# A fused token-mixing tower: in-block sums written by VectorE into the PSUM tile that TensorE accumulates, instead of being added by a permutation matmul

## The reference, cut to what matters

```
def step(state, qkv_t):
    q_t, k_t, v_t = qkv_t
    hebbian = jnp.einsum('bhi,bhj->bhij', v_t, k_t)
    state = retention[None] * state + Gamma[None] * hebbian
    y_t = jnp.einsum('bhij,bhj->bhi', W_static[None] + state, q_t)
    return (state, y_t)
...
h = _L0_tok_ref(x, ...)
h = h + _L0_attn_ref(_layernorm(h, axis=-1), ...)
h = h + _L0_ffn_ref(_layernorm(h, axis=-1), ...)
```

## Time and profile before

| | us |
|---|---|
| median of 3 runs (255.31 to 257.43) | 257.43 |
| the profiled execution, own time | 258.98 |
| its span in the trace | 257.1 |
| TensorE busy (granted clock 0.98 on the mean) | 227.3 |
| VectorE busy | 198.4 |
| GpSimd busy | 186.8 |
| ScalarE busy | 108.0 |

### The profile page before, as it was taken

One profiled execution on the slowest core, in us unless ns is written; L12 is line 12 of the kernel. 1 busy time (PEld: TensorE's weight loads), 2 busy tenths in 40 slices (PEclk: granted clock), 3 DMA queues, 4 the chain that ended last, 5 costly groups with the idle time before them and its releaser, 6 DMA issues.

```text
span 257.1 us, 7827 instructions
## 1 busy us (share of the span) xinstructions
PE 227.3 (88%) x3266; PEld 168.3 (65%) x3266; DVE 198.4 (77%) x391; ACT 108.0 (42%) x272; POOL 186.8 (73%) x97
## 2 busy tenths in 40 slices
PE   5998886998889999999989999998987965868993
PEld 5978644775558586776757767676554853547992
DVE  1027975688966896899799977887899989895773
ACT  6303674135522222697831056977102367100230
POOL 5870009999989999998599995776999999400031
PEclk9999999999999999999999999999999996899998
DMA  5492027411053921101640620025406100110002
GB/s 154 133 273 101 0 84 205 164 45 43 3 146 87 258 88 45 43 1 43 187 145 3 179 70 3 1 72 160 143 3 201 49 4 1 43 41 3 0 3 82
DMA packets 19443, 21.26 MB, mean 83 GB/s; under 512 B 2416, under 2 KB 13904, under 8 KB 19408
## 3 DMA queue, kind: packets, MB, share of 16 engines
q1 hardware_dynamic: 18640, 18.65, 23.3%
q0 software_dynamic: 768, 2.11, 3.4%
HBM read 14.98 MB, written 5.77 MB: 81 GB/s over the span
## 4 chain that ended last, share of the span: by engine, by line
PE 69%; DVE 13%; issue 6%; ACT 4%; DMA 3%; POOL 2%; another core or an unknown queue 1%; SPq 0%; DVEq 0%; ACTq 0%; POOLq 0%
PE y_ps L1127 10%; PE scr L978 10%; PE w_ps L1110 8%; PE scr L955 6%; PE q_ps L1072 5%; PE scr L992 5%; PE scr L1007 4%; PE scr L968 4%; PE scr L932 3%; PE y_ps L1072 3%; DVE zz L896 3%; PE scr L1031 3%; PE scr L1045 3%; POOL uu L447 2%; PE y_ps L1121 2%
## 5 line engine op out<-in xcount | busy, mean ns | idle before, releaser
L447 POOL TENSOR_TENSOR uu<-vg,kk 128x1024 f32<-128x1024 f32 x64 | 150.8, 2392 | 32.0 <-DMA vg<-v_far 19.3
L896 DVE TENSOR_TENSOR zz<-e_hg,q_ps 128x1524 f32<-128x1524 f32 x32 | 55.3, 1728 | 0.0
L867 DVE TENSOR_TENSOR_SCAN e_hg<-decay,w_ps 128x512 f32<-128x512 f32 x32 | 39.0, 1218 | 10.3 <-PE w_ps L1110 9.8
L1110 PE MATMUL w_ps<-uu,comb 128*32 128x128 f32 x1024 | 35.3, 277 | 1.5 <-POOL uu L447 1.1
L1110 PEld LDWEIGHTS w_ps<-uu,comb 128*32 128x32 f32 x1024 | 27.5, 111 | 9.0 <-issue 7.9
L1127 PEld LDWEIGHTS y_ps<-zz,coll 128*32 128x32 f32 x768 | 19.8, 111 | 19.4 <-issue 8.7
L1127 PE MATMUL y_ps<-zz,coll 128*32 128x128 f32 x768 | 28.2, 281 | 4.7 <-DVE zz L896 4.7
L406 POOL TENSOR_TENSOR tok_dom<-tok_dom,bf 128x1024 f32<-128x1024 f32 x4 | 8.7, 2186 | 21.0 <-DVE tmp_b L710 21.0
L527 ACT ACTIVATE junk<-tok_dom 128x256 bf16<-128x256 f32 x24 | 9.7, 407 | 28.6 <-DVE tok_dom L664 28.6
L882 DVE TENSOR_TENSOR zz<-e_hg,q_ps 128x512 f32<-128x512 f32 x32 | 21.7, 679 | 0.0
L396 POOL DMA_INDIRECT tok_dom<-in_table,ids_sb x16 | 15.5, 969 | 6.2 <-issue 3.5
(11 more groups left out here) (124 smaller groups left out, 390.5 us busy)
## 6 DMA issues: line engine op xcount, KB each, us to landing
vg<-v_far SPq DMA_DIRECT2D x32, 256.0 KB, 4.2
v_far<-v_sb SPq DMA_DIRECT2D x8, 256.0 KB, 4.0
out_h<-tok_dom SPq DMA_DIRECT2D x8, 256.0 KB, 2.1
k_far<-kk SPq DMA_DIRECT2D x12, 128.0 KB
k_sb<-k_far SPq DMA_DIRECT2D x4, 384.0 KB, 3.2
wexp<-in_w_exp SPq DMA_DIRECT2D x1, 256.0 KB
tok_dom<-in_table,ids_sb POOLq DMA_INDIRECT x16, 5.0
wproj<-in_w_proj SPq DMA_DIRECT2D x1, 256.0 KB
```

Source lines behind the costliest of these rows:

```text
L447: pool.tensor_tensor(uu[:, g % NU, two], v_of.to_broadcast(shape), k_of.to_broadcast(shape), ALU.mult).then_inc(s_u, 1)
L867: dve.tensor_tensor_scan(states(g).rearrange("p a m -> p (a m)"), decay[:, NA * n:NA * (n + 1)].rearrange("p a m -> p (a m)"), w.rearrange ...
L896: dve.tensor_tensor(z, e.to_broadcast(shape), q.to_broadcast(shape), ALU.mult).then_inc(s_z, 1)
L1110: last = pe.matmul(w_ps[32 * hp:32 * hp + 32, g % NW, a], comb[:, NA * n + a, hp], uu[:, g % NU, hp, a], start=True, stop=True, skip_group ...
```

## The change

`gv0` and `gv1` write their products and sums straight into `y_ps`, and set its last stream to zero (L828 of the kernel after). The static matmul comes after them, with start=False, and adds to what stands there; it waits for `s_gv`. `gv0` waits for `s_yt`, the copy of the unit before. `fix`, `order`, `lag_ps` and `s_fix` go; `qk` waits for `pair1` of the unit before instead. v takes y's channel order in its weights, and `copy_v` brings the rows into `v_far` in the old order, with four DMAs of 32 partitions. One matmul over all of `y_ps` (`clear`) is issued near the start, where four of eight `wake` matmuls were. All calendars are new. At the end `wake` 3.5 and 3.3 (eight matmuls) are gone.

```
-    58: q 2.0, pair0 1.1; 59: pair1 1.1; 60: fix 1.1; ...
+    55: pair0 1.1; 57: q 2.0, pair1 1.1, ffn 0.0; 59: xq_t 0.1; 61: ffn 0.1; ...
...
             def copy_v(c, hg):

                 taken(sp, "v", c, hg)
-                sp.dma_start(v_far[HG * c + hg].rearrange("o ch m -> ch o m"),
-                             v_sb[:, c % 2, hg, :].rearrange("p (o m) -> p o m", o=BLK)).then_inc(s_v4[hg], 16)
+                for a in range(NA):
+                    rows_of = slice(P // NA * a, P // NA * (a + 1))
+                    sp.dma_start(v_far[HG * c + hg].rearrange("o (r a) m -> a r o m", a=NA)[a],
+                                 v_sb[rows_of, c % 2, hg, :].rearrange("p (o m) -> p o m", o=BLK))\
+                      .then_inc(s_v4[hg], 16)
...
                 if c or hg:
-                    dve.wait_ge(s_fix, HG * c + hg)
+                    filled(dve, "pair1", c if hg else c - 1, 1 - hg)
...
                     if i == 0:
-                        dve.tensor_tensor(lag[:, 0:3 * MB], scr[:, bank, 0:3 * MB], v_sb[:, c % 2, hg, 0:3 * MB],
+                        if c or hg:
+                            dve.wait_ge(s_yt, HG * c + hg)
+                        dve.memset(y_ps[:, 3 * MB:], 0.0)
+                        dve.tensor_tensor(y_ps[:, 0:3 * MB], scr[:, bank, 0:3 * MB], v_sb[:, c % 2, hg, 0:3 * MB],
                                           ALU.mult).then_inc(s_free[bank], 1)
                         return
-                    dve.tensor_tensor(lag_ps[:, 0:2 * MB], scr[:, bank, 0:2 * MB], v_sb[:, c % 2, hg, 0:2 * MB],
+                    dve.tensor_tensor(lag[:, 0:2 * MB], scr[:, bank, 0:2 * MB], v_sb[:, c % 2, hg, 0:2 * MB],
                                       ALU.mult).then_inc(s_dve, 1)
...
-                    link(dve.tensor_tensor(lag[:, MB:3 * MB], lag_ps[:, 0:2 * MB], lag[:, MB:3 * MB], ALU.add))
+                    link(dve.tensor_tensor(y_ps[:, MB:3 * MB], y_ps[:, MB:3 * MB], lag[:, 0:2 * MB], ALU.add))
...
+            def clear(*_):
+
+                pe.matmul(y_ps[:], idf[:], wexp[:].rearrange("p k e -> p (k e)"), start=True, stop=True)
...
                     taken(pe, "q", c, hg)
-                    pe.matmul(y_ps[:], wst[:, hg, :], q_sb[:, hg, :], start=True, stop=True)
+                    pe.wait_ge(s_gv, HG * c + hg + 1)
+                    pe.matmul(y_ps[:], wst[:, hg, :], q_sb[:, hg, :], start=False, stop=True, skip_group_check=True)
```

127 lines of the change are left out of this document (58 added, 69 removed).

## The result

The changed kernel takes 268.94 us (268.00 to 271.66, four runs) beside 256.8 us (255.31 to 257.43) of the kernel before on the same chip: a ratio of 1.050, interval 1.041 to 1.059 (the two medians alone give 1.047). The forecast was 257.7 us, hardly a change (+0.3), with a range to 261.5; the measured time lies 7 us above that range. Ratios and intervals are over the fast runs of each kernel, those not over 1.5% above its fastest.

What follows compares the result with a forecast made beforehand. GpSimd was taken to bound up to about 89 us, TensorE to 186, VectorE to 233. Start 0, two middle chunks +1.3, last chunk 0 and end -1.0 gave +0.3: 257.7 us, range 253.6 to 261.5.

Steps and rivals of the forecast that it cites:

- GpSimd's start: At the start, four DMAs for one copy of v make GpSimd begin later: +0.8 us, between +0.6 and +1.6.
- rounds 8 to 24, four `fix`: TensorE stage, chunks 1 and 2: four `fix` matmuls of 0.65 us go, worth 2.6 us, 1.3 per chunk.
- waits of today: TensorE stage: TensorE's present idle time of 1.15 us in 50 goes under the new order, -1.2 us per chunk.
- norm wait (`tmp_f`): Before the next chunk's transposes: less cover and `moments2` in ScalarE's norm make TensorE wait, +2.4 us per chunk (0 to +4.3).
- `s_gv` wait: At unit (c, 1) the static matmul waits for `gv1` with only `ffn` between: +0.75 us per chunk.
- the end: Before the last `ffn`: with four `wake` matmuls instead of nine, `ffn` and everything behind it come 1.0 us sooner.
- two new waits: TensorE stage: TensorE waits for the next chunk's norm, +2.4 us, and for `s_gv`, +0.75 us, per chunk.
- my second rival: TensorE stage: the new wait reaches some 3 us, TensorE's clock falls in both chunks; +5, or 262.5 us; chance 0.10.
- combine(8) stays where it is: Start of the TensorE stage: later GpSimd and new waits leave combine(8) unmoved, 0 us, between -0.4 and +1.0.
- The last chunk: VectorE's queue sets it: memsets +0.3, `ffn` wait gone -1.2, `stat2` wait +0.9; sum 0, give or take 1 us.
- The condition of the faster one: Norm covered in the TensorE stage: `moments2` costs TensorE at most 0.6 us per chunk, giving 254.1 us; chance 0.27.
- The slower one, the handshake over `y_ps`: VectorE reaches `gv0` one product late at unit (c, 1), `s_gv` costs 2.4: +3.4, 261.1 us; chance 0.11.

Runs made afterwards that it cites:

- chip 3: A later chip where the kernel before and the changed kernel were both run again unchanged: ratio 1.026.
- e4_again: Kernel before with its old data flow under all five calendars of the changed kernel, second run, on chip 3: 1.033 of before.
- e13: Kernel before without eight of its `wake` matmuls at the end (3.5 ahead of the last `ffn`, 3.3 behind it): 0.995 of before.
- before_again: Kernel before, unchanged, run and profiled again on chip 2: median 257.8 us.
- e3: Changed kernel with v copied out in one DMA per half chunk instead of four, leaving out the reordering of v's rows: 1.033 of before.
- e1: Changed kernel with SP's copies of v of chunks 2 and 3 put back to the slots of the kernel before: 1.028 of before.
- after_third: Changed kernel, unchanged, run again on chip 3: 1.026 of before.
- e12: Changed kernel with old slots for SP's v copies, ScalarE's `moments2` halves and GpSimd's last gathers, and stores of chunks 0 and 1 two slots later: 1.022 of before.
- e2: Changed kernel with ScalarE's first `moments2` half of chunks 0 and 1 moved behind the transposed-input copies of chunks 2 and 3: 1.033 of before.
- e9: Kernel before's data flow with the changed kernel's TensorE and VectorE orders, its ScalarE, SP and GpSimd orders partly put back: 1.039 of before.
- after_again: Changed kernel, unchanged, run again on chip 2: 1.037 of before.

## Why the prediction was wrong

By its own steps, with the first pair of profiles:

| step | forecast | measured |
|---|---|---|
| GpSimd's start | +0.8 | +0.58 (38.56 for 37.98), chip 3 +0.77; not passed on to round 0 |
| up to round 8 | 0 (-0.4 to +1.0) | +5.2; chip 3 +2.6; e4_again +0.4 |
| rounds 8 to 24, four `fix` | -2.6 | -2.6 |
| waits of today | -2.4 | -2.3: both are gone |
| norm wait (`tmp_f`) | +4.8 | +3.6 |
| `s_gv` wait | +1.5 | +0.6 |
| not in the sum | 0 | q's copy +2.8, longer busy time of the same matmuls +1.1, clock +1.6 |
| rounds 24 to 31 | 0, give or take 1 | +2.3 |
| the end | -1.0 | -1.1 at its place; the stretch -0.4, with +1.6 of clock; e13 -1.2 to -1.4 for eight matmuls |

**What was right.** GpSimd's start, the end of the stage's old waits, the 1.0 us of `wake` matmuls at the end, and the two new waits by name and place; by size both were set too high (2.4 for 1.8 and 0.75 for 0.3 us per chunk). The first transposes were to come 6.7 us after `corr` 2.1 and came 120.07 - 113.82 = 6.25 after it. The memset took 0.17 us on PSUM too and not 0.25:

```profile
85.52 0.17 DVE L828 MEMSET y_ps<- 128x128 f32 x1 [4.44 <-PE scr L1011]
85.59 0.50 DVE L829 TENSOR_TENSOR y_ps<-scr,v_sb 128x384 f32<-128x384 f32 x1
```

The rule of the Trainium skill (VectorE: DVE Perf Modes, Why PSUM operands drop a tier) gives VectorE's read ports as its reason. The prediction applied it to a memset, which reads nothing, and by it expected more time; the trace shows no such difference.

**What failed.** The step "two new waits, which I get by walking the new order" took the rest of the new order as free. In rounds 8 to 24 the sum missed 5.5 us of it. One part is a wait that the walk passed over: `attn` and `ffn` now come right behind q and `pair1` and need the scratch bank that ScalarE is still copying q from, 0.7 us at each of four places (L1025 and L1057, `<- ACT q_ps`). A second is that the same matmuls keep TensorE busy 1.1 us longer in the new order; the sum took a matmul's time as the same in every order. The third is the clock, my second rival. It was right in kind and wrong in its point: after 1.45 us of idling, followed by 0.36, the clock fell to 0.58, and the same 1.44 in chunk 3 did not lower it (`combine` 1.08 us behind it). The row on which the point rested, 1.82 us at 194.58 with full clock, is one execution's: in before_again the same wait did lower it. A threshold read from one row isn't one. (The rival's own time is off by 0.2 as well: 257.7 + 5 is 262.7.)

**Up to round 8** the failed step is "combine(8) stays where it is". The bounds allowed for GpSimd's start and forgot everything else. Of the 5.2 us, 2.6 are there without the stutter (chip 3, 47.04 for 44.44), but only 0.4 in e4_again and e3 and 0.7 in e1, so that some 2 us belong to after_third's own execution. In all of after_third, e1 and e3 TensorE waits for GpSimd ahead of round 7 (2.20, 1.91 and 1.61 us), a wait which the new orders bring; in after_third alone the clock falls behind it (0.75 from 82 to 88 us), for 1.6 us. The rest of the 5.2 is stutter and clock. This was not to be had from the trace of before, in which the stutter is hidden in rounds 4 to 5 and costs 1 us. But the range could have allowed for it: one profile doesn't show what a stretch costs elsewhere.

**The last chunk** was given 0. Its new waits are GpSimd's (4.4 us, with its stop behind the stores), `gv1`'s before the static matmul of unit (3, 1) (2.0) and q's copy (0.7), and VectorE's product ends 1.0 us more of TensorE's waits; against them stand 4.1 us less for the quantised input and its transposes, and 1.8 us less busy time. e12 takes the first away without gain, since the wait for the quantised input comes back (4.2 us), and which of the order's edits lengthens the stretch by 2.3 us is open.

**The rivals.** The condition of the faster one, that `moments2` costs TensorE no more than 0.6 us per chunk, was about met: without it (e2) the waits for `tmp_f` are 1.3 us shorter in two chunks, and the stage 0.3 us, apart from the clock. Its 254.1 us didn't follow, since the time was lost elsewhere. The slower one, the handshake over `y_ps`, had the right mechanism and the wrong case: in the changed kernel it costs 3.0 us in all; under the old orders it costs 17. I weighed how long the new wait lasts and not what the orders pay for keeping it short.

**Open.** Which move in the new calendars carries the 4.2 us, whose parts are given with e9: `attn` and `ffn` right behind q and `pair1` account for 2.8 us of waits, but that move wasn't tried alone in the kernel before. Open too are the stutter's cause, and why the clock falls behind a wait in one execution and not in the next.

## What to carry to other kernels

When an edit takes work from a bound engine and adds a dependence at the front of a stage, price the dependence first under the old order: here some 26 us, as I placed the steps, for 5 us of matmuls. The new order that hides it must be charged with everything that it moves, and where a sum takes the rest as free, that term needs bounds as wide as the waits of a whole stage. Before a difference of 1 or 2 us is put down to an edit, look whether the clock fell in one of the two profiles. A long idle time of an engine that is rounds ahead (11.24 us of GpSimd) is no cause until taking it away alone shortens the stretch; compare stretches between marks of the program, not totals, when chips differ by 1%.

## What was not expected of the hardware

TensorE's stutter: the 24 matmuls of a collect, 0.84 us elsewhere, in handfuls with gaps of 0.3 us and no releaser, between rounds 4 and 6 on some chips and never on others. And the granted clock: in after 0.58 for 4 us behind a wait of 1.45 us in one chunk and 1.00 behind one of 1.44 us in the next; in after_third the other way round; in after_again 1.00 behind both. Behind one wait of 1.82 us it was 1.00 in before and 0.57 in before_again.
